# Two attention layers behind a non-local block, split fp32 on one core: shared SBUF regions padded so that large matmul operands begin at 128 modulo 256 bytes

## The chip, the cores and the metric

The kernel runs on one core of a Trainium2 chip. The metric is the device time of one execution in microseconds (us). On-chip memory (SBUF) has 128 partitions; an "address" below is the byte offset of a tensor within a partition, the same in all 128. In the names of this text PE is TensorE, DVE VectorE, ACT ScalarE, POOL GpSimd, and SP the engine that issues the DMAs.

## What is computed

The input is x of 8 batches with 256 tokens of 512 numbers, and a context of the same shape. Cut to what matters:

```python
# first: linear attention over the channels, batch norm folded, residual
W  = einsum('bnc,bcm->bnm', theta_x, phi_x) / 512
x0 = bn(conv(w_w, einsum('bnm,bmc->bnc', W, g_x))) + x
# then (x0 and ctx read as 4 chunks of 512 tokens x 512): two cross-attentions, H=16 heads, K=128
h  = layer_norm(x) * scale + offset
q  = h @ wq + bq ; k, v = ctx @ wk + bk, ctx @ wv + bv    # and one more key and value, bias_k, bias_v
x  = x + softmax(q @ k.T / sqrt(128)) @ v @ wo + bo
# last: an MLP, F=2048
x  = x + gelu(layer_norm(x) @ w_fc1 + b_fc1) @ w_fc2 + b_fc2
```

## The kernel before

Every large product is made of three fp32r matmuls. An operand A is kept as a high part and a low part, A = hi + lo, and `product` (lines 581 to 584) adds lhs.hi x rhs.hi (L582), lhs.hi x rhs.lo (L583) and lhs.lo x rhs.hi (L584) into one PSUM bank. `lhs` is the stationary operand (128 columns, loaded into the array by a weight load of its own, 512 bytes per partition), `rhs` the moving one (512, 258 or 256 columns of 4 bytes). A row of the profile names them as out<-in, both inputs after the arrow; the weight load of the next matmul runs while the present one streams.

The work runs in three stages, in an order that Python writes out by hand (`FRONT`, `SLOTS`, `last_order`), the same for all engines:

- **Front** (K and V of all heads of both layers, into DRAM): `keys` multiplies `wks` (stationary) by `cT` (moving, the transposed context), `values` multiplies `cT` (stationary) by `wvs` (moving). ACT and DVE write the split result into `stage`, four slots in turn, and SP stores each slot to `kd` or `vd`. The non-local block is woven in between.
- **Attention** (64 steps of 4 items each, an item being one head of one 256-token half): `projected` makes q of the next step (stationary `wqs` for even groups of heads, `wqs_b` for odd, moving `hT`), `logits` multiplies `qT` (stationary) by a key block `kb` (moving, 258 columns), `turn` transposes the probabilities, `weighted` multiplies a value block `vb` (stationary) by `PT` (moving, 256 columns), and `output` multiplies `oT` (stationary) by `wos` (moving, 512). Key and value blocks come back from DRAM into two buffers each, `kb0`/`kb1` and `vb0`/`vb1`.
- **Tail** (MLP, 32 steps): `projected` again (`wqs` or `wqs_c` by turns, four steps each) and `output` with `gT0` or `gT1` by turns of one step (stationary) and `wos` or `wos_c` by turns of four steps (moving).

Six stretches of SBUF are shared by tensors that live at different times. `region(name, size)` (line 200) allocates one, and `at(first, size, ...)` (line 204) lays tensors out in it one behind the other. Each tensor or region starts where the one before it ends, so that a region's size decides the addresses of all that come after. `x` starts at byte 16512, which is 128 modulo 256; `turned_rows`, `raw0`, `raw1` and `weights_a` have sizes that are multiples of 256, and so start at 128 as well. `weights_b`, `staged` and `block_0` have 16512 bytes, 128 over a multiple of 256, and halves of 8256 bytes, 64 over one.

Of the kernel before, what the change touches and what calls it, by code (L numbers as in the profile page):

```python
# [28 lines left out]
F32 = mybir.dt.float32  # L29
F32R = mybir.dt.float32r  # L30
# [4 lines left out]
B, TOK, D = 8, 256, 512  # L35
# [5 lines left out]
CH = D // P  # L41
# [144 lines left out]
def bass_xattn(nc, x_in, ctx_in, thw, thb, pgw, pgb, www, bncol, wa, wk, wv, wb, hcol, vrow,  # L186
               lncol, f1col, orow, out):
    ctx = ExitStack()
    with ctx:
        def sb(name, shape, dt=F32):  # L190
            return ctx.enter_context(nc.sbuf_tensor(name, [P, *shape], dt))

        def sem(name):
            return ctx.enter_context(nc.semaphore(name))
# [4 lines left out]

        def region(name, size):  # L200

            return sb(name, [size // 4]), nc.sbuf_base - size

        def at(first, size, *tensors):

            made, where = [], first
            for name, shape, dt in tensors:
                made.append(nc.alloc_sbuf_tensor_at(name, [P, *shape], dt, offset=where))
                where += 4 * int(np.prod(shape))
            assert where <= first + size  # L210
            return made


        x = sb("x", [TILES, D])
        assert (nc.sbuf_base - 4 * TILES * D) % 64 == 0
        _, r = region("turned_rows", 65536)
        cT, hT = at(r, 65536, ("cT", [2, CH, 2048], F32R)) + at(r, 65536, ("hT", [2, CH, 2048], F32R))
        raw = [sb(f"raw{i}", [CH, 256]) for i in range(2)]
        _, r = region("weights_a", 16384)
        (wks,) = at(r, 16384, ("wks", [2, CH, 512], F32R))  # L220
        wqs, wos = at(r, 16384, ("wqs", [2, CH, 256], F32R), ("wos", [2, 2, D], F32R))
        _, r = region("weights_b", 16512)
        (wvs,) = at(r, 16512, ("wvs", [2, CH, 512], F32R))
        kb1, vb1 = at(r, 8256, ("kb1", [2, 2, 516], F32R)) + at(r + 8256, 8256, ("vb1", [2, 4, 256], F32R))
        wqs_c, wos_c = at(r, 8256, ("wqs_c", [2, CH, 256], F32R)) + at(r + 8256, 8256, ("wos_c", [2, 2, D], F32R))
        _, r = region("staged", 16512)
        (stage,) = at(r, 16512, ("stage", [4, 2, 516], F32R))
        (PT,) = at(r, 8256, ("PT", [2, 2, 512], F32R))
        (oT,) = at(r + 8256, 8256, ("oT", [2, 2, 512], F32R))
        _, r = region("block_0", 16512)  # L230
        kb0, vb0 = at(r, 8256, ("kb0", [2, 2, 516], F32R)) + at(r + 8256, 8256, ("vb0", [2, 4, 256], F32R))
        xb, pg, th, wm, msb = at(r, 16512, ("xb", [2, D], F32), ("pg", [4, 256], F32), ("th", [D], F32),
                                 ("wm", [TOK], F32), ("msb", [P], F32))
        gT = at(r, 8256, ("gT0", [2, 2, 512], F32R)) + at(r + 8256, 8256, ("gT1", [2, 2, 512], F32R))
        _, r = region("queries", 8192)
        (qT,) = at(r, 8192, ("qT", [2, 2, 512], F32R))
        wth, wpg, www_s, pgb_s = at(r, 8192, ("wth", [2, CI], F32), ("wpg", [2, 2 * CI], F32), ("www_s", [TOK], F32),
# [3 lines left out]
        _, r = region("spare", 10240)  # L241
# [42 lines left out]
        unit, free, hi, staged = sem("unit"), sem("free"), sem("hi"), sem("staged")  # L284
# [896 lines left out]
```

## Time and profile before

| | |
|---|---|
| median of 3 runs | 2394.86 us (2382.49 to 2408.23) |
| the profiled execution | 2395.99 us, span of its instructions 2394.1 us |
| PE busy | 2351.6 us, 98% |
| PE weight loads | 1997.9 us, 83% |
| DVE busy | 1339.3 us, 56% |
| ACT busy | 1143.8 us, 48% |
| POOL busy | 462.4 us, 19% |
| granted clock of PE | 0.996 of full speed |

Each matmul of `product` has three lines, L582 to L584, by which the profile groups them. The end of a matmul is modelled by the profiler, so durations of neighbours overlap: a matmul of 512 columns shows about 0.39 us and its successor starts 0.23 us after it. The distance from start to start is what counts for time.

### The profile page before, as it was taken

How to read it: one execution, taken by the hardware profiler on the slowest of the kernel's cores; microseconds unless marked ns; L12 is line 12 of the kernel's file. 1: busy time of each engine (PE TensorE's matmuls, PEld its weight loads, DVE VectorE, ACT ScalarE, POOL GpSimd, SP SyncE). 2: the span in 40 equal slices, each digit the busy share in tenths (PEclk: the TensorE clock that was granted, in tenths of full speed). 3: DMA queues.
4: the chain of work that ended last, by engine and by line, in shares of the span. 5: the costliest groups of instructions: out<-in, count | busy, mean ns of one | idle time of the engine just before them, and what ended most of it. 6: DMA issues, size and time to landing. Idle time of an engine off the chain costs nothing.

```text
span 2394.1 us, 32423 instructions
## 1 busy us (share of the span) xinstructions
PE 2351.6 (98%) x12304; PEld 1997.9 (83%) x12304; DVE 1339.3 (56%) x2328; ACT 1143.8 (48%) x2717; POOL 462.4 (19%) x280
## 2 busy tenths in 40 slices
PE   8999999999999899999999989999999999999999
PEld 7888888888888788888888878888888887788887
DVE  4544445445445666666666676666666666644433
ACT  3222222222223566666666677666666667422222
POOL 2121112112123501111001244111001115611110
PEclk9999999999999999999999999999999999999999
DMA  7555656566556424333333333333333331100001
GB/s 272 197 196 203 230 195 215 202 217 227 191 203 212 168 98 143 127 115 136 125 137 124 124 107 119 133 116 134 126 139 124 123 134 45 44 18 27 27 1 70
DMA packets 142168, 331.83 MB, mean 139 GB/s; under 512 B 8896, under 2 KB 74944, under 8 KB 125632
## 3 DMA queue, kind: packets, MB, share of 16 engines
q1 hardware_dynamic: 141296, 329.68, 39.3%
q8 instruction: 99, 1.62, 0.3%
q14 instruction: 53, 0.43, 0.1%
q10 hardware_dynamic: 720, 0.10, 0.0%
HBM read 190.81 MB, written 138.94 MB: 138 GB/s over the span
## 4 chain that ended last, share of the span: by engine, by line
PE 90%; DVE 4%; ACT 4%; DMA 1%; issue 1%; POOL 1%; ACTq 0%; SPq 0%; DVEq 0%; POOLq 0%
PE U L582 23%; PE U L584 23%; PE U L583 23%; PE T L676 4%; PE O L582 2%; PE O L584 2%; PE O L583 2%; PE S L584 2%; PE S L583 2%; PE S L582 2%; DVE hT L1005 1%; ACT aff L815 1%; DVE gT L1015 1%; ACT probs L856 1%; ACT hT L818 1%
## 5 line engine op out<-in xcount | busy, mean ns | idle before, releaser
L1024 DVE TENSOR_TENSOR x<-x,U 128x512 f32<-128x512 f32 x384 | 260.9, 683 | 79.9 <-PE U L584 77.5
L848 ACT ACTIVATE probs<-S,nm 128x257 f32<-128x257 f32 x512 | 237.7, 476 | 37.4 <-DVE nm L1032 37.4
L1032 DVE TENSOR_REDUCE nm<-S 128x2 f32<-128x514 f32 x256 | 177.3, 692 | 123.6 <-PE S L584 119.8
L866 ACT ACTIVATE PT<-T 128x512 fp32r<-128x512 f32 x256 | 152.5, 596 | 173.9 <-PE T L676 173.4
L856 ACT ACTIVATE probs<-probs,rs 128x256 f32<-128x256 f32 x512 | 230.1, 500 | 1.4 <-DVE rs L1036 1.1
L797 ACT ACTIVATE stage<-U,hc 128x512 fp32r<-128x512 f32 x128 | 88.1, 689 | 286.9 <-PE U L584 286.9
L989 DVE SCALAR_TENSOR_TENSOR stage<-U,hc,stage 128x512 fp32r<-128x512 f32 x128 | 96.2, 751 | 223.4 <-ACT stage L797 223.4
L582 PE MATMUL U<-cT,wks 128*128 128x512 f32 x512 | 214.0, 418 | 2.0 <-DVE cT L967 2.0
L582 PE MATMUL U<-wos,oT 128*128 128x512 f32 x512 | 214.2, 418 | 0.4 <-DVE oT L1047 0.4
L804 ACT ACTIVATE stage<-tmp 128x512 fp32r<-128x512 f32 x128 | 81.0, 633 | 271.1 <-DVE tmp L997 271.1
L1047 DVE SCALAR_TENSOR_TENSOR oT<-O,hc,oT 128x256 fp32r<-128x256 f32 x256 | 123.8, 484 | 147.5 <-ACT oT L875 147.3
L464 POOL CAST wos<-raw 128x1024 fp32r<-128x1024 f32 x20 | 20.8, 1039 | 954.1 <-PE U L584 954.1
L584 PE MATMUL U<-wos,oT 128*128 128x512 f32 x512 | 203.0, 397 | 0.0
L583 PE MATMUL U<-wos,oT 128*128 128x512 f32 x512 | 202.1, 395 | 0.0
L582 PE MATMUL U<-wvs,cT 128*128 128x512 f32 x512 | 201.7, 394 | 0.0
L584 PE MATMUL U<-cT,wks 128*128 128x512 f32 x512 | 200.4, 391 | 0.0
L583 PE MATMUL U<-cT,wks 128*128 128x512 f32 x512 | 200.2, 391 | 0.0
L584 PE MATMUL U<-wvs,cT 128*128 128x512 f32 x512 | 199.4, 390 | 0.0
L583 PE MATMUL U<-wvs,cT 128*128 128x512 f32 x512 | 199.4, 389 | 0.0
L1040 DVE TENSOR_TENSOR PT<-T,PT 128x512 fp32r<-128x512 f32 x256 | 175.5, 685 | 42.3 <-ACT PT L866 42.3
L875 ACT ACTIVATE oT<-O,hc 128x256 fp32r<-128x256 f32 x256 | 121.2, 473 | 130.8 <-PE O L584 130.6
L676 PE MATMUL T<-ident,probs 128*128 128x128 f32 x1024 | 155.3, 274 | 13.5 <-ACT probs L856 13.4
(166 smaller groups left out, 5827.1 us busy)
## 6 DMA issues: line engine op xcount, KB each, us to landing
kd<-stage SPq DMA_DIRECT2D x128, 516.0 KB, 3.1
kb<-kd SPq DMA_DIRECT2D x64, 1032.0 KB, 4.8
vd<-stage SPq DMA_DIRECT2D x128, 512.0 KB, 3.2
vb<-vd SPq DMA_DIRECT2D x64, 1024.0 KB, 5.0
raw<-wa SPq DMA_DIRECT2D x24, 512.0 KB, 5.9
raw<-wb SPq DMA_DIRECT2D x24, 512.0 KB, 5.9
raw<-wk SPq DMA_DIRECT2D x16, 512.0 KB, 5.9
raw<-wv SPq DMA_DIRECT2D x16, 512.0 KB, 5.7
```

The costliest lines, as they stand in the source:

```text
L582: pe.matmul(o, lhs[0], rhs[0], start=start, stop=False)
L583: pe.matmul(o, lhs[0], rhs[1], start=False, stop=False)
L584: return pe.matmul(o, lhs[1], rhs[0], start=False, stop=stop)
L676: mm = pe.transpose(T[:, at_:at_ + P], probs[:, J % 2, qt, tt * P:tt * P + P], ident[:])
L848: ins = act.activation(probs[:, r, qt, 0:257], S[:, qt, 0:257], ACT.Exp, bias=nm[:, r, qt:qt + 1], scale=-1.0, accum_out=sums[:, r, qt:qt ...
L856: ins = act.activation(probs[:, r, qt, 0:256], probs[:, r, qt, 0:256], ACT.Copy, scale=rs[:, r, qt:qt + 1])
L866: act.activation(PT[:, J % 2, 0, :], T[:], ACT.Copy).then_inc(pt_hi, 1)
L875: act.activation(oT[:, 0, h, b * 256:b * 256 + 256], O[:, 0:256], ACT.Identity, bias=hc[:, 3, at_:at_ + 1]).then_inc(o_hi, 1)
L1024: dve.tensor_tensor(x[:, tile, :], x[:, tile, :], bank(what, s, t), ALU.add).then_inc(free, 1)
L1032: dve.tensor_reduce(nm[:, J % 2, :], S[:, :, 0:257], AX.X, ALU.min).then_inc(least, 1)
L1040: dve.tensor_tensor(PT[:, J % 2, 1, :], T[:], f(PT[:, J % 2, 0, :]), ALU.subtract).then_inc(pt, 1)
L1047: dve.scalar_tensor_tensor(out=oT[:, 1, h, to], in0=O[:, 0:256], scalar=hc[:, 3, at_:at_ + 1], in1=f(oT[:, 0, h, to]), op0=ALU.add, op1=AL ...
```

## The change

Three regions grow from 16512 to 16640 bytes, which is a multiple of 256, and the tensors in them change places so that a tensor of 8192 bytes comes first and one of 8256 or 8192 second, with nothing between. `region` now asserts that what it made starts at 128 modulo 256. No instruction is added, removed or moved: every engine issues the same operations on the same shapes in the same order with the same waits. Only addresses differ. They come out as follows, in bytes modulo 256:

| tensor | used as | before | after |
|---|---|---|---|
| cT, hT, wks, wvs, wqs, wqs_c, wos, x, raw | both kinds | 128 | 128 |
| kb0, kb1 (moving; their rows have 2064 bytes) | first row | 128 | 128 |
| vb0, vb1 | stationary | 192 | 128 |
| wos_c | moving | 192 | 128 |
| PT | moving | 0 | 128 |
| oT | stationary | 64 | 128 |
| gT0 / gT1 | stationary | 128 / 192 | 128 / 128 |
| qT | stationary | 0 | 128 |
| wqs_b | stationary | 0 | 128 |
| stage, z, aff, tmp, probs | not of `product` | 0 | 128 |
| ident (moving of the transposes) | | 32 | 160 |

A slice of a tensor other than `kb` begins a multiple of 256 bytes behind the tensor's start, so the table holds for each matmul. A row of `kb` is 516 numbers, 2064 bytes or 16 over a multiple of 256, and the second batch half starts 1032 bytes (8 over) further: the eight slices that `logits` reads from it start at 128, 136, 144, 152, 160, 168, 176 and 184, before and after.

```diff
         def region(name, size):
 
-            return sb(name, [size // 4]), nc.sbuf_base - size
+            made = sb(name, [size // 4])
+            assert (nc.sbuf_base - size) % 256 == 128
+            return made, nc.sbuf_base - size
...
-        _, r = region("weights_b", 16512)
-        (wvs,) = at(r, 16512, ("wvs", [2, CH, 512], F32R))
-        kb1, vb1 = at(r, 8256, ("kb1", [2, 2, 516], F32R)) + at(r + 8256, 8256, ("vb1", [2, 4, 256], F32R))
-        wqs_c, wos_c = at(r, 8256, ("wqs_c", [2, CH, 256], F32R)) + at(r + 8256, 8256, ("wos_c", [2, 2, D], F32R))
-        _, r = region("staged", 16512)
-        (stage,) = at(r, 16512, ("stage", [4, 2, 516], F32R))
-        (PT,) = at(r, 8256, ("PT", [2, 2, 512], F32R))
-        (oT,) = at(r + 8256, 8256, ("oT", [2, 2, 512], F32R))
-        _, r = region("block_0", 16512)
-        kb0, vb0 = at(r, 8256, ("kb0", [2, 2, 516], F32R)) + at(r + 8256, 8256, ("vb0", [2, 4, 256], F32R))
-        xb, pg, th, wm, msb = at(r, 16512, ("xb", [2, D], F32), ("pg", [4, 256], F32), ("th", [D], F32),
+        _, r = region("weights_b", 16640)
+        (wvs,) = at(r, 16640, ("wvs", [2, CH, 512], F32R))
+        vb1, kb1 = at(r, 16640, ("vb1", [2, 4, 256], F32R), ("kb1", [2, 2, 516], F32R))
+        wos_c, wqs_c = at(r, 16640, ("wos_c", [2, 2, D], F32R), ("wqs_c", [2, CH, 256], F32R))
+        _, r = region("staged", 16640)
+        (stage,) = at(r, 16640, ("stage", [4, 2, 516], F32R))
+        PT, oT = at(r, 16640, ("PT", [2, 2, 512], F32R), ("oT", [2, 2, 512], F32R))
+        _, r = region("block_0", 16640)
+        vb0, kb0 = at(r, 16640, ("vb0", [2, 4, 256], F32R), ("kb0", [2, 2, 516], F32R))
+        xb, pg, th, wm, msb = at(r, 16640, ("xb", [2, D], F32), ("pg", [4, 256], F32), ("th", [D], F32),
                                  ("wm", [TOK], F32), ("msb", [P], F32))
-        gT = at(r, 8256, ("gT0", [2, 2, 512], F32R)) + at(r + 8256, 8256, ("gT1", [2, 2, 512], F32R))
+        gT = at(r, 16640, ("gT1", [2, 2, 512], F32R), ("gT0", [2, 2, 512], F32R))[::-1]
```

## Rows read from the trace of the kernel before

**Rows 1.** The page: the chain that ended last, by engine, as shares of the span.
```profile
PE 90%; DVE 4%; ACT 4%; DMA 1%; issue 1%; POOL 1%; ACTq 0%; SPq 0%; DVEq 0%; POOLq 0%
```
**Rows 2.** Busy time of PE by stretch: instructions, granted clock, DMA share, GB/s.
```profile
0.00:50.00 50.00, 41.12 (x198) 1.00 0.79 283
50.00:800.00 750.00, 748.68 (x3304) 1.00 0.58 206
800.00:850.00 50.00, 38.03 (x206) 0.86 0.34 127
850.00:2050.00 1200.00, 1186.10 (x7128) 1.00 0.35 122
2050.00:2394.00 344.00, 337.71 (x1473) 1.00 0.09 31
```
**Rows 3.** Waits of PE, longest first: us in total, times, longest.
```profile
PE T L676 <- ACT probs L856: 13.4, 16, 2.9
PE S L716 <- DMA x<-ctx_in: 6.8, 1, 6.8
PE U L619 <- DVE hT L1005: 6.0, 1, 6.0
```
**Rows 4.** Line L583 on PE: duration in ns, minimum/median/maximum, first and last start.
```profile
L583 PE MATMUL U<-cT,wks x512: 387/389/628, 13.1 to 739.3; 128*128 128x512 f32 x171
L583 PE MATMUL U<-wvs,cT x512: 387/389/397, 63.4 to 792.9; 128*128 128x512 f32 x171
L583 PE MATMUL S<-kb,qT x512: 278/282/420, 784.0 to 2017.2; 128*128 128x258 f32 x171
L583 PE MATMUL O<-PT,vb x512: 276/279/416, 800.7 to 2031.7; 128*128 128x256 f32 x171
L583 PE MATMUL U<-wos,oT x512: 387/392/632, 810.0 to 2037.0; 128*128 128x512 f32 x171
L583 PE MATMUL U<-hT,wqs x384: 387/389/398, 766.4 to 2335.5; 128*128 128x512 f32 x192
L583 PE MATMUL U<-hT,wqs_b x256: 387/393/404, 870.9 to 1997.5; 128*128 128x512 f32 x128
```
**Rows 5.** Lines L584 and L582 on PE, same columns.
```profile
L584 PE MATMUL U<-wos,oT x512: 387/394/632, 810.2 to 2037.2; 128*128 128x512 f32 x171
L582 PE MATMUL U<-wos,oT x512: 388/397/776, 809.7 to 2036.7; 128*128 128x512 f32 x171
```
**Rows 6.** Timeline of PE in the tail: start us, duration us, instruction.
```profile
2313.98 0.39 PE L582 MATMUL U<-wos,gT 128*128 128x512 f32 x1
...
2319.42 0.39 PE L582 MATMUL U<-hT,wqs 128*128 128x512 f32 x1
...
2324.86 0.40 PE L582 MATMUL U<-wos,gT 128*128 128x512 f32 x1
...
2330.46 0.39 PE L582 MATMUL U<-hT,wqs 128*128 128x512 f32 x1
```
**Rows 7.** Timeline of PE later in the tail, `wos_c` moving.
```profile
2357.87 0.40 PE L582 MATMUL U<-wos_c,gT 128*128 128x512 f32 x1
...
2363.38 0.40 PE L582 MATMUL U<-hT,wqs_c 128*128 128x512 f32 x1
...
2368.87 0.39 PE L582 MATMUL U<-wos_c,gT 128*128 128x512 f32 x1
...
2374.35 0.39 PE L582 MATMUL U<-hT,wqs_c 128*128 128x512 f32 x1
```
**Rows 8.** The page: DMA issues from SP, KB each, median us to landing.
```profile
vd<-stage SPq DMA_DIRECT2D x128, 512.0 KB, 3.2
```
**Rows 9.** Waits of the SP queue: us in total, times, longest.
```profile
SPq L409 <- DVE stage L1000: 290.9, 127, 7.9
```

## The prediction

> **What bounds the kernel now.** I read first the chain that ended last: PE holds 90% of it [rows 1]. The table by stretch says where PE is not busy: 8.9 us in the first 50 us, 1.3 us in the rest of the front, 12.0 us at the change of stage near 800 us, 13.9 us in the attention and 6.3 us in the tail [rows 2]. The list of PE's waits puts names to them: in total 13.4 us for the probabilities, 6.8 us for the first input, 6.0 us for `hT` [rows 3]. None of these is a steady wait: 16 waits for the probabilities among 256 items are an exception, not the rule. So the kernel's time is the number of matmuls times the distance at which PE starts them, plus about 42 us of gaps. A change that leaves all instructions where they are can act only on that distance (or on the gaps).
>
> **What the distance depends on.** The three lines of a product do the same work on different operands, so their durations can be compared across operands. A duration is the distance to the next start plus a constant: in the tail 24 matmuls `hT,wqs` take 2324.86 - 2319.42 = 5.44 us, 226.7 ns each, and show 389 ns, so the constant is 162 ns [rows 4, 6]. With it, the medians of line L583 (the middle one of a product, whose successor never waits for another engine) sort by address. Where both operands begin at 128 modulo 256 (`cT,wks`, `wvs,cT`, `hT,wqs`), the median is 389 ns, in the front and in the attention alike. `hT,wqs_b` differs from `hT,wqs` only in its stationary tensor, at 0 instead of 128, and takes turns with it in the same loop: 393. `wos,oT`, stationary at 64: 392, and 394 on L584 [rows 4, 5].
>
> The tail has the cleanest comparison, since the same code runs with four pairs of addresses. A step of 24 matmuls from `gT0` (128) with `wos` (128) takes 2319.42 - 2313.98 = 5.44 us; from `gT1` (192) with `wos` (128) 5.60 us [rows 6]. With `wos_c` (192) it takes 5.51 us from `gT0` (128) and 5.48 us from `gT1` (192) [rows 7]. So 128 with 128 is the fastest pair, 192 with 192 nearly so, and unequal residues cost 3 to 7 ns per matmul. This is a real property of where operands lie, of 1 to 3%, and not noise of a wait: none of these steps waits.
>
> The Trainium skill (SBUF — State Buffer, section "SBUF: two separate sides") says that PE never waits on anyone for SBUF, and lists a second, independent read port for weight loads. Taken literally, a matmul's rate could not depend on addresses, and the sum would be 0. The rows on `wqs` and `wqs_b` speak against that reading, and I go by the rows; the rule stays as the second rival below.
>
> **The change part by part.** Against the profiled execution's own 2395.99 us, 1.1 us above the median of the runs:
>
> 1. `cT,wks`, `wvs,cT`, `hT,wqs`, `hT,wqs_c`: same addresses, nothing. That is the whole front (800 us).
> 2. `hT,wqs_b`: 256 x 3 = 768 matmuls, 393 to 389 ns: 768 x 4 = **3.1 us**.
> 3. `wos,oT`: 512 x 3 = 1536 matmuls. L583 gives 3 ns, L584 5 ns; L582's median of 397 mixes in first matmuls of a group, which are late for other reasons. I take 4 ns: **6.1 us**; bounds 3 ns (4.6) and the mean of all three, (8 + 3 + 5) / 3 = 5.3 ns (8.2) [rows 4, 5].
> 4. `gT` in the tail: 32 steps, eight of each pair. Against 5.44 us: 8 x 0.16 + 8 x 0.07 + 8 x 0.04 = **2.2 us** [rows 6, 7].
> 5. `PT,vb`: 1536 matmuls of 256 columns, now 0 with 192, then 128 with 128. No row shows 256 columns with both at 128. Half of 227 ns plus the constant gives 275.5 ns, and the minimum of the row is 276. From 279: 3.5 x 1536 = **5.4 us**. Lower bound: none. I take the full value, as 276 does occur in this row [rows 4].
> 6. `kb,qT`: 1536 matmuls of 258 columns. The same scaling gives 276.4 ns against 282, or 5.6 x 1536 = 8.6 us at most. But only `qT` moves, from 0 to 128; of the eight slices of `kb` seven still start 8 to 56 bytes past 128, so equal residues come about in one of eight. Between 0 and 8.6 I take a quarter, **2.2 us**, since a difference of 8 to 56 bytes is smaller than the 64 that cost `oT` its 3 ns [rows 4].
> 7. Transposes: operands keep their distance (both move by 128). Nothing.
> 8. DMA: `stage` slots start at 0, 32, 64, 96 before and 128, 160, 192, 224 after, and `vb` moves from 192 to 128. What covers a slower store is the ring of four slots: a unit of V is 12 matmuls or 2.7 us, so a slot is needed again after 10.9 us, and the store lands 3.2 us after issue [rows 8]. The queue itself waits for its data, 290.9 us in all [rows 9]. A store would have to take twice as long before PE noticed. Nothing. (The Trainium skill, DMA: Bandwidth & Descriptors, "How a descriptor splits into AXI transactions", says that a descriptor not at a 256-byte boundary costs an extra transaction; by it one slot in four would get 17 for 16 of them. No row here shows that, and the cover above is wide enough for it.)
> 9. ACT, DVE and POOL: the same operations; they are busy for half of the time and PE waits for them rarely [rows 3]. If PE's slot shrinks by 19 us in 1200 us, by 1.6%, their slack does not end.
>
> Sum: 3.1 + 6.1 + 2.2 + 5.4 + 2.2 = 19.0 us. The profiled execution would come to 2377.0, the median of the runs to 2375.9; I say **2376 us**, 0.8% less. The lower end of the sum without the two terms of the short matmuls is 3.1 + 4.6 + 2.2 = 9.9 us (2385); the upper end with all ceilings is 3.1 + 8.2 + 2.2 + 5.4 + 8.6 = 27.5 us (2367).
>
> **Rivals.** (a) The full effect: what counts is that both operands lie within the same stretch, not that they begin at the same byte, so that `kb,qT` reaches 276 ns too. For it: the spread of 278 to 282 to more in its row looks like that of `PT,vb`. Against: seven of eight slices stay unequal. Gain 27.5 us, 2367 us. (b) Nothing: the differences between rows are those of tensors or of places in the code, not of residues, as a rule that PE never waits for SBUF would have it. For it: address pairs are few, and no row has 256 columns at 128 with 128. Against: `gT0` and `gT1` run the same code. 2395 us. (c) Slower: ACT and DVE now write `PT`, `oT`, `qT`, `tmp`, `probs` and `z` all at the residue at which PE reads, where before they were spread over 0, 64 and 192, and each write near PE's read costs it some ns. Its place is the attention stage, with 6,144 matmuls there besides the transposes; it needs 19.0 / 6144 = 3 ns each to undo the gain and 43 / 6144 = 7 ns to make the kernel 1% slower (2419 us). Against it: `hT,wqs` in the attention, amid the same writers, has the same median of 389 as `wvs,cT` in the front [rows 4].
>
> **How the numbers follow.** The likeliest case, a gain of 10 to 24 us, has 0.58; (a) 0.22; (b) 0.15; (c) 0.05. A measurement of this kernel can tell about 1% from no change, which is 24 us, and its three runs lie up to 13 us off their median; this noise is the larger part of my range. Faster by over 1% (below 2371 us) is (a) and the upper edge of the likeliest case: 0.27. Slower by over 1%: 0.04. The rest, 0.69, is within 1%. The range runs from 2361 us, the full effect with some noise, to 2394 us, where the likeliest case's lower end with noise and half of (b) lie.
>
> **What would show it.** In the changed kernel's trace the medians of `hT,wqs_b`, `wos,oT` and all `wos,gT` and `wos_c,gT` on L583 and L584 should be 389 to 390 ns, and tail steps 5.44 us each whatever the buffer. `PT,vb` should fall from 279 to 276; `kb,qT` from 282 to about 281, to 276 under (a). The front's rows must not move. Under (b) `wqs_b` stays at 393; under (c) `hT,wqs` rises above 389 in the attention. If the rows fall as said and the time does not, PE's waits for the probabilities will have grown instead, and I have misjudged the slack.

## The result, and the profile after

The changed kernel takes 2405.5 us (median of 22 runs, 2394.5 to 2408.4), the kernel before 2396.2 us (22 runs beside them, 2382.5 to 2408.2). The ratio is 1.0035, with a 95% interval from 1.0023 to 1.0047: slower by 9.3 us in the medians and by 8.4 us (0.35%) in the ratio, where 2376 us was forecast, and above the upper end of the range (2394 us). The profiled execution takes 2407.6 us, 11.6 us more than that of before.

The times of both kernels come in three groups about 10.5 us apart, near 2386, 2396 and 2407 us, and the result can't be understood without them. Before has 5, 16 and 1 of its 22 runs in them; after has none in the first, 10 in the second (2394.5 to 2400 us) and 12 in the third.

The page of after: busy time, then the chain that ended last.
```profile
PE 2354.0 (98%) x12304; PEld 2003.0 (83%) x12304; DVE 1349.6 (56%) x2328; ACT 1145.0 (48%) x2717; POOL 462.6 (19%) x280
...
PE 89%; DVE 4%; ACT 4%; issue 1%; DMA 1%; POOL 1%; ACTq 0%; SPq 0%; DVEq 0%; POOLq 0%
```
The chain looks like [rows 1]. DVE is busy 10.3 us longer with the same instructions (1339.3 before), and that is the first hint. Busy time of PE by stretch after (columns as in [rows 2]), and then two narrower windows:
```profile
0.00:50.00 50.00, 41.02 (x197) 1.00 0.78 282
50.00:800.00 750.00, 748.60 (x3303) 1.00 0.60 206
800.00:850.00 50.00, 38.04 (x207) 0.86 0.34 128
850.00:2050.00 1200.00, 1177.67 (x7072) 0.99 0.35 121
...
1450.00:1470.00 20.00, 10.39 (x59) 0.75 0.23 80
1470.00:1490.00 20.00, 19.41 (x108) 0.91 0.34 113
```
The front and the change of stage near 800 us are as in [rows 2]. In the attention PE is idle for 22.3 us where it was 13.9 us. One place holds nearly all of the difference: between 1450 and 1470 us PE works 10.4 us of 20. The same two windows of before:
```profile
1450.00:1470.00 20.00, 18.22 (x106) 0.91 0.22 70
1470.00:1490.00 20.00, 20.00 (x121) 1.00 0.44 159
```
The waits of PE after, longest first, name what it waited for there. They stand against [rows 3]: the wait of 6.0 us for `hT` has become two, 14.1 us together, and the wait for the probabilities is as it was.
```profile
PE U L620 <- DVE hT L1006: 14.1, 2, 8.1
PE T L677 <- ACT probs L857: 12.7, 15, 2.8
PE S L717 <- DMA x<-ctx_in: 6.9, 1, 6.9
```
The lines are one higher than before (the `assert`): the middle matmul of a product is L584 now. Its durations after (minimum/median/maximum), to be read against [rows 4] and [rows 5]:
```profile
L584 PE MATMUL U<-cT,wks x512: 387/389/632, 13.2 to 739.9; 128*128 128x512 f32 x171
...
L584 PE MATMUL S<-kb,qT x512: 277/282/420, 784.6 to 2030.0; 128*128 128x258 f32 x171
L584 PE MATMUL O<-PT,vb x512: 277/283/415, 801.3 to 2044.3; 128*128 128x256 f32 x171
L584 PE MATMUL U<-wos,oT x512: 387/393/628, 810.6 to 2049.5; 128*128 128x512 f32 x171
L584 PE MATMUL U<-hT,wqs x384: 387/393/398, 767.0 to 2347.5; 128*128 128x512 f32 x192
L584 PE MATMUL U<-hT,wqs_b x256: 389/393/398, 871.5 to 2010.3; 128*128 128x512 f32 x128
L584 PE MATMUL U<-wos,gT x128: 387/389/628, 2054.1 to 2363.8; 128*128 128x512 f32 x128
```
Four of the five forecast gains are not there: `wqs_b` stays at 393, `oT` goes from 392 to 393, `kb,qT` stays at 282, and `PT,vb` goes the wrong way, 279 to 283. `hT,wqs`, whose addresses did not change, rises from 389 to 393. Only the tail does as forecast. Its timeline after, where each row is the first matmul of a step:
```profile
2326.22 0.39 PE L583 MATMUL U<-wos,gT 128*128 128x512 f32 x1
...
2331.66 0.39 PE L583 MATMUL U<-hT,wqs 128*128 128x512 f32 x1
...
2369.74 0.39 PE L583 MATMUL U<-wos_c,gT 128*128 128x512 f32 x1
...
2375.18 0.39 PE L583 MATMUL U<-hT,wqs_c 128*128 128x512 f32 x1
```
A step takes 5.44 us from either buffer and with either weights, where [rows 6] and [rows 7] have 5.44 to 5.60 us. (Six steps at a change of weights take 5.86 us in after and 5.84 or 5.85 us in before, with a wait of 0.1 us in them.)

### The profile page after: what moved, and what is told of

It is laid out like the page before. It is cut to its first block, busy times and chain, and to the rows that moved or that the text cites. A ratio compares the mean times of both kernels' runs of the same rounds, so it can differ in the third digit from the quotient of the medians.

```text
span 2405.7 us, 32423 instructions
## 1 busy us (share of the span) xinstructions
PE 2354.0 (98%) x12304; PEld 2003.0 (83%) x12304; DVE 1349.6 (56%) x2328; ACT 1145.0 (48%) x2717; POOL 462.6 (19%) x280
## 4 chain that ended last, share of the span: by engine, by line
PE 89%; DVE 4%; ACT 4%; issue 1%; DMA 1%; POOL 1%; ACTq 0%; SPq 0%; DVEq 0%; POOLq 0%
PE U L583 23%; PE U L584 23%; PE U L585 23%; PE T L677 4%; PE O L585 2%; PE O L584 2%; PE O L583 2%; PE S L585 2%; PE S L583 2%; PE S L584 2%; DVE hT L1006 2%; ACT aff L816 1%; ACT probs L857 1%; DVE gT L1016 1%; ACT hT L819 1%
## 5 line engine op out<-in xcount | busy, mean ns | idle before, releaser
L583 PE MATMUL U<-cT,wks 128*128 128x512 f32 x512 | 214.2, 418 | 2.1 <-DVE cT L968 2.1
L583 PE MATMUL U<-wos,oT 128*128 128x512 f32 x512 | 214.7, 419 | 0.2 <-DVE gT L1016 0.2
L584 PE MATMUL U<-wos,oT 128*128 128x512 f32 x512 | 202.6, 396 | 0.0
L583 PE MATMUL U<-wvs,cT 128*128 128x512 f32 x512 | 201.8, 394 | 0.0
L584 PE MATMUL U<-cT,wks 128*128 128x512 f32 x512 | 200.4, 391 | 0.0
L584 PE MATMUL U<-wvs,cT 128*128 128x512 f32 x512 | 199.3, 389 | 0.0
```

What stands on the lines that cost most here:

```text
L583: pe.matmul(o, lhs[0], rhs[0], start=start, stop=False)
L584: pe.matmul(o, lhs[0], rhs[1], start=False, stop=False)
```

## Where the time went: one instruction of DVE that can't get in

Laid over each other, start by start, the two traces are 0.5 us apart at 730 us, 2.0 us at 1426 us and 12.4 us at 1458 us; from there they stay together (12.8 us at 2010 us). The start of the tail adds about 1 us, and its steps give about 2 us back. So 10.4 us of the 11.6 us arise within some 30 us of time. Timeline of after there, first DVE and POOL at the start of the first layer's attention, then at the start of the second layer's, and PE:
```profile
829.61 10.49 DVE L1006 TENSOR_TENSOR hT<-aff,hT 128x512 fp32r<-128x512 f32 x1 [1.64 <-ACT hT L819]
...
824.71 14.84 POOL L537 TENSOR_TENSOR x<-x,brow 128x512 f32<-128x512 f32 x12
...
1453.86 11.84 DVE L1006 TENSOR_TENSOR hT<-aff,hT 128x512 fp32r<-128x512 f32 x1 [1.64 <-ACT hT L819]
...
1449.32 14.85 POOL L537 TENSOR_TENSOR x<-x,brow 128x512 f32<-128x512 f32 x12
1464.13 1.03 POOL L465 CAST wqs_b<-raw 128x1024 fp32r<-128x1024 f32 x1
...
1465.76 1.11 PE L620 MATMUL U<-ident,z 128*128 128x128 f32 x4 [8.12 <-DVE hT L1006]
```
The subtraction that makes the low part of `hT` takes 0.69 us elsewhere, where POOL is idle. Here it takes 10.49 and 11.84 us, and nothing else of DVE runs. POOL meanwhile adds the output bias to `x`, twelve times without a gap. At 829 us DVE ends 0.55 us after POOL's row (824.71 + 14.84 = 839.55, and 829.61 + 10.49 = 840.10). At 1453 us it ends 0.54 us after the cast that follows the row (1465.16 and 1465.70), so it was let in at the first pause that POOL made. PE stands for 8.12 us. Its granted clock is at the lower level of 1.2 GHz (0.50 of full speed) from 1460 us, within this stall, until 1473 us, after it: that is the 0.75 and 0.91 in the windows above.

The same places in the timeline of before:
```profile
829.13 10.46 DVE L1005 TENSOR_TENSOR hT<-aff,hT 128x512 fp32r<-128x512 f32 x1 [1.64 <-ACT hT L818]
...
1451.10 1.50 DVE L1005 TENSOR_TENSOR hT<-aff,hT 128x512 fp32r<-128x512 f32 x1 [1.64 <-ACT hT L818]
...
1456.22 1.79 DVE L1005 TENSOR_TENSOR hT<-aff,hT 128x512 fp32r<-128x512 f32 x1 [1.17 <-ACT hT L818]
...
1445.75 15.86 POOL L536 TENSOR_TENSOR x<-x,brow 128x512 f32<-128x512 f32 x12
```
The first layer had the same lock-out, and it was already the 6.0 us wait of [rows 3]. In the second layer DVE got in twice between two additions, after 1.50 and 1.79 us, and POOL's row became 1.0 us longer (15.86 for 14.84).

The Trainium skill (SBUF — State Buffer, section "Who interferes with whom") says that a DVE instruction with two SBUF inputs contends with a GpSimd instruction that reads SBUF, and that the later one is blocked for the whole instruction. Both traces agree that it is blocked. The second layer of before fits this as it stands, since DVE got in at the end of the addition that it had met. The lock-outs go further: DVE is blocked for a row of up to nine instructions of about 1.25 us, not for one.

One lock-out costs about 10 us, and the groups of times would be executions with none, one and two of them. This is theory A. It says that the addresses decide little by themselves, and that they may act through the moment at which DVE arrives. Theory B is that the new addresses cost time directly: at PE (rival (c) of the prediction, writers near PE's reads), or at DVE, POOL and ACT.

## Experiments

**Are lock-outs the difference?** In both kernels each of POOL's twelve additions in the first two layers waits for an item of the attention, so that they lie apart; `queries` moves behind the first four so that its weights don't come late.

```diff
                 for t in range(4 * c, 4 * c + 4):
+                    if c and n < LAYERS:
+                        pool.wait_ge(logit, n * BODIES * CHUNKS * 4 + t - 3)
                     pool.tensor_tensor(x[:, t, :], x[:, t, :], brow[:], ALU.add).then_inc(ln_bias, 1)
...
-                if E:
+                if E and E != BODIES:
                     queries(E + 1)
...
                         add_bias(n, c)
+                        if c == 1 and n < LAYERS:
+                            queries(E + 2)
```

With the addresses of before:

> The addresses of before, but GpSimd's twelve bias additions at the start of a layer no longer run back to back: each waits for the logits of one item, and the query weights that stood behind them are split earlier. Theory 1 (the loss of the changed kernel is a second DVE instruction that is locked out for 10 us behind GpSimd's additions, and not a slower rate of matmuls): no DVE instruction takes over 3 us at the start of a layer, PE's long waits for hT go, the time falls by 10 to 12 us below the median of before, to about 2385 us, with a spread of runs of under 4 us. Theory 2 (the loss comes from the matmul rate): the additions have nothing to do with it; the time stays within 3 us of before.

With the addresses of after:

> The same spaced additions with the addresses of after. Theory 1: about 2386 to 2388 us, 1 to 3 us above the kernel with spaced additions and the addresses of before (the sum of the steady differences between the two traces), and 18 to 20 us below the changed kernel's 2405.5. Theory 2: it stays 8 to 9 us above the other, whatever that one's time is.

Measured: 2392.5 us with the addresses of before (12 runs, ratio to before 0.9983, interval 0.9970 to 0.9995), and 2392.1 us with those of after (0.9983, 0.9973 to 0.9994). The spread shrinks from 26 us to 8 us with the addresses of before, and from 14 us to 4 us with those of after. The 9 us between the kernels are gone, which is what theory A says and theory B excludes. But the level is not what was expected: 2385 us and a spread under 4 us had been forecast for the first, and it fell by 3.8 us alone. Waits of PE for `hT` in the kernel with after's addresses, against 14.1 us above, and its timeline of DVE at the first layer:
```profile
PE U L624 <- DVE hT L1010: 1.1, 1, 1.1
...
828.15 5.35 DVE L1010 TENSOR_TENSOR hT<-aff,hT 128x512 fp32r<-128x512 f32 x1 [1.64 <-ACT hT L823]
```
One shorter lock-out is left in each, 5.35 us here and 5.85 us with the addresses of before, behind the first additions, which still run in a row. It would account for the missing part of the fall, and the last experiment below takes it away. So the 9 us between the kernels hang on the lock-outs and not on what the addresses do elsewhere: theory A.

**Can the lock-out be aimed?** If the moment of arrival decides, shifting POOL's row should turn the cases round. A scratch addition of 320 columns ahead of the second layer's row in before, of 160 columns in after (shown for before; the scratch tensor is also cleared once at the start):

```diff
+        idle = sb("idle", [320])
...
+                    if n == 1:
+                        pool.tensor_tensor(idle[:], idle[:], idle[:], ALU.add)
                     for c in range(1, CHUNKS):
                         add_bias(n, c)
```

> Addresses of before; one more GpSimd instruction, an addition over 320 scratch columns (about 0.8 us), stands ahead of the twelve bias additions at the start of the second layer and shifts them against DVE by 0.8 us. Theory 1 (whether DVE is locked out is decided by where in an addition of GpSimd's it arrives; in the trace of before 0.35 us after one's start, and it got in; in that of after 0.80 us, and it did not): DVE now meets the additions at another point, 0.8 us earlier in their row, that is near the end of one, and is locked out in most runs; the median goes from 2396 to about 2406 us, as in the changed kernel, with no address changed. Theory 2 (addresses cause the loss): within 2 us of before.

> Addresses of after; the extra GpSimd instruction has 160 columns (about 0.45 us) and moves the additions so that DVE arrives 0.35 us after the start of one, as in the trace of before. Theory 1: mostly the lower of the changed kernel's two groups of times, median about 2397 us. Theory 2: the changed kernel's 2405 us or more.

Measured: 2395.8 us (12 runs, ratio 0.9999, 0.9980 to 1.0019) and 2405.7 us (12 runs, 1.0040, 1.0024 to 1.0055). About 2406 and 2397 us had been expected, and neither came. The delayed before was merely spread over the groups: 4 runs at 2386 to 2387 us, 6 at 2394 to 2398 and 2 at 2408. Its profiled execution happened to be one of the fastest, 2387.0 us, and its timeline of DVE shows no long lock-out in either layer:
```profile
829.52 1.44 DVE L1009 TENSOR_TENSOR hT<-aff,hT 128x512 fp32r<-128x512 f32 x1 [1.64 <-ACT hT L822]
...
1447.40 1.81 DVE L1009 TENSOR_TENSOR hT<-aff,hT 128x512 fp32r<-128x512 f32 x1 [1.17 <-ACT hT L822]
```
The timeline of DVE in the delayed after (profiled at 2404.9 us) has both, the second as:
```profile
1451.04 12.09 DVE L1010 TENSOR_TENSOR hT<-aff,hT 128x512 fp32r<-128x512 f32 x1 [1.64 <-ACT hT L823]
```
So the count of lock-outs accounts for the groups (2387.0 with none, 2396.0 for before with one, 2404.9 and 2407.6 with two), but my model of when one happens was wrong. In the traces of all the kernels here DVE got in whenever it came within 0.04 us of an addition's start. Between 0.35 and 0.41 us it went either way, in the two layers of a single execution even. At about 0.20, at 0.54, at 0.68 and from 0.79 to 1.25 us it was shut out, but at 0.93 us it once got in, amid a row. So the moment of arrival within an addition does not decide it.

**What do the addresses do to PE alone?** 56 phases of 24 matmuls each are appended to before, each matmul complete in itself, on data that is there and with results that nobody uses; the stationary and the moving operand start at 0, 64, 128 or 192. In the last 24 phases ACT and DVE write beside them, at residue 0 or 128.

```diff
+            for p, (n, rw, rm, near) in enumerate(PHASES):
+                pe.wait_ge(act_at, p)
+                pe.wait_ge(dve_at, p)
+                for i in range(24):
+                    mm = pe.matmul(S[:, i % 2, 0:n], hT[:, 0, i % 4, start_of(rw):start_of(rw) + P],
+                                   hT[:, 1, i % 2, start_of(rm):start_of(rm) + n], start=True, stop=True)
```

> The kernel of before, followed by 56 phases of 24 matmuls on hT, each phase with one residue of the stationary and one of the moving operand (0, 64, 128, 192), first with 512 and then with 256 columns and nothing else running, then six pairs of residues with ACT and DVE writing to SBUF at residue 0 or at 128. Theory own operands: at 512 columns equal residues take 227 ns, others 229 to 236; at 256 columns with both at 128 it takes 120 ns even with ACT and DVE idle, unequal ones 113 to 117. Theory neighbours: alone, all 256-column pairs take 113 to 114 ns, and 120 appears only beside ACT and DVE, above all at the same residue.

The kernel took 2642.7 us with its phases. Durations by phase, each row over the window of one phase (up to two matmuls of the phase before it are in). L775 is the line of the phases. The pairs are stationary, moving: (0,0), (0,64), (0,128), (64,0) with 512 columns; then (0,64), (128,64), (128,128) with 256.
```profile
L775 PE MATMUL S<-hT x24: 389/389/472, 2384.4 to 2389.7; 128*128 128x512 f32 x24
L775 PE MATMUL S<-hT x25: 388/392/398, 2389.7 to 2395.2; 128*128 128x512 f32 x25
L775 PE MATMUL S<-hT x26: 390/394/404, 2395.2 to 2401.0; 128*128 128x512 f32 x26
...
L775 PE MATMUL S<-hT x25: 390/394/394, 2406.4 to 2412.0; 128*128 128x512 f32 x25
...
L775 PE MATMUL S<-hT x25: 279/279/283, 2475.8 to 2478.7; 128*128 128x256 f32 x25
...
L775 PE MATMUL S<-hT x26: 276/276/280, 2498.4 to 2501.3; 128*128 128x256 f32 x26
L775 PE MATMUL S<-hT x26: 274/283/283, 2501.2 to 2504.1; 128*128 128x256 f32 x26
```
From start to start, over the last 21 of each phase, 512 columns take 227 ns where both residues are equal (226.7 to 228.5, whichever residue it is), 229 where the moving one is 64 higher, and 232 to 233 in the other two cases. That is the effect that the prediction read from the tail, and it is real. With 256 columns the order turns round. Equal residues are the slowest, 119.6 to 119.8 ns; 128 apart gives 118.4 to 118.7; 64 apart gives either 117.8 or 113.3 to 114.1, and the two are not a matter of the pair: (64,128) takes 117.8 alone and once beside the writers, and 113.3 in its other phase beside them. In the 24 phases with ACT and DVE writing beside PE, at 0 or at 128, no pair is slower than alone by more than 1 ns ((128,128) with 512 columns takes 227.2 and 227.8, against 228.2 alone). So writers that store at the residue at which PE reads cost it nothing here, which is what rival (c) needed.

The phase (128,128) with 512 columns also shows how long that takes. Its distances run 228, 229, 234, 236, 224, 231, 235, 229, 232, 231, and only then 227, 226, 227; (64,64) and (192,192) settle after five. A product in the attention is issued in groups of 6 between shorter matmuls, a step of the tail in groups of 24. In the attention of after, `hT,wqs` and `hT,wqs_b`, all at 128 now, both run through their six matmuls at 234, 233, 231, 230, 230 and 229 ns on average (from each start to the next): the products have equal residues there, and are over before the pace has settled.

**Do the residues of `PT` and `vb` count in the kernel?** Three kernels with the addresses of before except: `vb` at 0 as `PT` is, `vb` alone at 128, and `PT`, `oT` and `vb` all at 128 (this one with one more wait of ACT at the start, since `PT` then overlaps a third slot of `stage`). The lines are shown for `vb0`; `vb1` moves alike.

```diff
-        kb0, vb0 = at(r, 8256, ("kb0", [2, 2, 516], F32R)) + at(r + 8256, 8256, ("vb0", [2, 4, 256], F32R))
+        kb0, vb0 = at(r, 8256, ("kb0", [2, 2, 516], F32R)) + at(r + 8320, 8192, ("vb0", [2, 4, 256], F32R))  # both at 0
+        vb0, kb0 = at(r, 16512, ("vb0", [2, 4, 256], F32R), ("kb0", [2, 2, 516], F32R))  # 0 with 128, both at 128
+        (PT,) = at(r + 128, 8256, ("PT", [2, 2, 512], F32R))  # both at 128
+        (oT,) = at(r + 8320, 8256, ("oT", [2, 2, 512], F32R))
```

> Addresses of before, except vb0 and vb1: at 0 instead of 192, so that PT,vb has 0 with 0. Theory own operands, as in the phases (256 columns with equal residues settle at 120 ns): the mean distance of PT,vb goes from 116.3 to between 118 and 119, near the 118.6 of the changed kernel, its L584 and L583 medians from 279 to 282 or 283. If only 128 with 128 were slow: it stays at 279.

> Addresses of before, except vb0 and vb1 at 128 (PT stays at 0), half way round. The phases have 118.7 ns for this pair when it runs long; so PT,vb should lie between before and the changed kernel, at 117.5 to 118.7 ns.

> Addresses of before, except PT, oT, vb0 and vb1, all at 128; qT, wqs_b, z, aff, probs and the tail as before. Own operands: PT,vb as in the changed kernel (mean distance 118.6 ns, medians 280 to 283); wos,oT about 231.0 as in the changed kernel, and not 227. hT,wqs rises too if what a group of six inherits from the short matmuls before it counts, since neither its own operands nor qT change.

One run each: 2412.1, 2400.4 and 2402.5 us. The kernel with both at 0 has two long lock-outs (11.28 and 11.90 us), the other two kernels one. Line L583 in the kernel with both at 128, and then of `hT,wqs` in the kernel where `vb` alone moved, to 128:
```profile
L583 PE MATMUL O<-PT,vb x512: 274/282/415, 800.8 to 2038.2; 128*128 128x256 f32 x171
L583 PE MATMUL U<-wos,oT x512: 387/393/628, 810.1 to 2043.5; 128*128 128x512 f32 x171
...
L583 PE MATMUL U<-hT,wqs x384: 387/393/398, 765.0 to 2339.9; 128*128 128x512 f32 x192
```
A mean distance below is taken from start to start, without the stretches of low clock; another way of averaging moves it by up to 1 ns. The mean distance of `PT,vb` is 118.4 ns at equal residues (at 0 and at 128 alike), 118.6 with 0 and 128, and 116.3 in before, 64 apart. These 2 ns times 1536 are 3.3 us; with one lock-out each, the two kernels lie 4.4 and 6.5 us above the 2396.0 of before. `wos,oT` with both at 128 stays at 393, so the third term of the prediction fails on its own too. And `hT,wqs` goes from 389 to 393 in all three, though neither its operands nor any tensor that ACT, DVE or POOL write moved in the kernels with `vb` alone. So the rise of `hT,wqs` in after comes from the matmuls of `PT,vb` between its groups, and not from writers beside PE.

**Do the other tensors' addresses matter?** The addresses of after with 128-byte pads that put `z`, `aff` and `probs` back to 0. (`tmp` and `wqs_b` stay at 128, since the region that holds them does.)

```diff
+        pad0 = sb("pad0", [32])
         z = sb("z", [4, D])
         aff = sb("aff", [2, 512])
+        pad1 = sb("pad1", [32])
...
+        pad2 = sb("pad2", [32])
         probs = sb("probs", [2, 2, 258])
```

> The changed kernel with z, aff and probs, which ACT and DVE write and which are no operands of a product, back at residue 0; all products as in the changed kernel. Theory neighbours (rival c of the prediction): hT,wqs in the attention falls back from its mean of 391.7 ns towards the 391.1 of before and its L584-to-be median from 393 to 389, and PT,vb from 281.5 back to 278.5. Theory own operands: both stay as in the changed kernel within 0.3 ns.

One run: 2405.5 us, with two lock-outs of 10.44 and 11.83 us. `PT,vb` stays at 282 to 283 ns on its three lines (279 in before) and `hT,wqs` at 390 to 394 (389 to 392 in before), so neither goes back, as it would under rival (c). The time lies in after's group, so these three tensors need not be at 128 for a second lock-out. One run does not tell how often it comes.

**A version that keeps the good part.** The spaced kernel with the addresses of before, where only the three tensors that end at equal residues with 512 columns move: `gT1` and `wos_c` in the tail, and `wqs_b`.

```diff
-        wqs_c, wos_c = at(r, 8256, ("wqs_c", [2, CH, 256], F32R)) + at(r + 8256, 8256, ("wos_c", [2, 2, D], F32R))
+        wqs_c, wos_c = at(r, 8256, ("wqs_c", [2, CH, 256], F32R)) + at(r + 8192, 8256, ("wos_c", [2, 2, D], F32R))
...
-        gT = at(r, 8256, ("gT0", [2, 2, 512], F32R)) + at(r + 8256, 8256, ("gT1", [2, 2, 512], F32R))
+        gT = at(r, 8256, ("gT0", [2, 2, 512], F32R)) + at(r + 8192, 8256, ("gT1", [2, 2, 512], F32R))
...
-        (wqs_b,) = at(r, 10240, ("wqs_b", [2, CH, 256], F32R))
+        (wqs_b,) = at(r + 128, 10112, ("wqs_b", [2, CH, 256], F32R))
```

> Spaced additions, addresses of before, and only three tensors moved to 128: gT1 and wos_c in the tail, wqs_b in the attention; PT, oT, qT, vb, stage, z, aff, tmp and probs stay. If residues act as the prediction had it for these three: 2.2 us less in the tail and 3 us less for wqs_b, 5 us below the kernel with spaced additions alone. If the rate in the attention depends on what ACT and DVE do beside PE, as the changed kernel's trace suggests: 2 us less from the tail, and between 0 and 2 us from wqs_b.

Measured: 2389.1 us (7 runs, ratio 0.9962, 0.9947 to 0.9977), 3.4 us less than the spaced kernel, within the 2 to 4 us of the second expectation and short of the 5 us of the first. `wqs_b` goes from 233.1 to 229.7 ns here, with `PT,vb` and `wos,oT` around it as before, and the tail's `wos,gT` and `wos_c,gT` are at 227.

**The last lock-out, first try.** All sixteen additions spaced; those of the first chunk go behind the normalisation of all four.

```diff
-                    if c and n < LAYERS:
-                        pool.wait_ge(logit, n * BODIES * CHUNKS * 4 + t - 3)
+                    if t and n < LAYERS:
+                        pool.wait_ge(logit, n * BODIES * CHUNKS * 4 + t)
...
             normalise(0, 1)
-            add_bias(0, 0)
             normalise(0, 2)
             queries(1)
             normalise(0, 3)
-            for c in range(1, CHUNKS):
+            for c in range(CHUNKS):
                 add_bias(0, c)
```

> The kernel with spaced additions and three tensors moved, and now all sixteen additions of a layer's start spaced by one item each and put behind the normalisation. In the kernel with twelve spaced, DVE still took 5.9 us for one hT at 829 us, behind the first four additions. Theory 1: that instruction falls to under 2.5 us, PE loses its low clock around 838 us, and the time falls by a further 4 to 7 us, to about 2383 us. Rival: GpSimd's normalisation of z holds the port as well and hT still waits; the time stays at 2389.

Measured: 2407.4 us (6 runs, ratio 1.0054, 1.0037 to 1.0072). Its waits of PE, and its timeline of DVE:
```profile
PE U L586 <- DVE hT L1009: 27.7, 3, 15.7
...
1453.08 0.69 DVE L1028 TENSOR_TENSOR x<-x,U 128x512 f32<-128x512 f32 x1 [10.96 <-POOL x L538]
1453.68 3.57 DVE L1009 TENSOR_TENSOR hT<-aff,hT 128x512 fp32r<-128x512 f32 x1
```
It had been expected at 2383 us. DVE adds the first outputs to `x` only when the bias of the whole chunk is in, and now waits 10.96 us for that. The two long stalls of PE (15.7 us at the first layer, 11.5 us at the second) are longer than those of a lock-out, and mostly from another cause: the first chunk's semaphore, which I had moved. A short lock-out of 3.57 us follows each of the waits.

**Second try.** Back to the three-tensor kernel, with only the waits of the twelve additions three items later:

```diff
-                        pool.wait_ge(logit, n * BODIES * CHUNKS * 4 + t - 3)
+                        pool.wait_ge(logit, n * BODIES * CHUNKS * 4 + t)
```

> Twelve spaced additions and three tensors moved, as in the kernel that took 2389.1 us, and each addition waits for the logits of three items more, so that the first three of them no longer follow the four additions ahead of them without a gap (in that kernel DVE's hT at 829 us took 6.4 us behind such a row). Theory 1: that hT falls under 2.5 us, no stall of PE for hT at 829 us, time 2384 to 2386 us, the level of the fastest runs of before. Theory 2 (the row has nothing to do with it): 2389 us.

Measured: 2382.8 us (5 runs, 2381.6 to 2385.2; ratio to before 0.9944, 0.9930 to 0.9957). It had been expected at 2384 to 2386 us. It beats both kernels, before by 13.3 us and after by 23 us; about 3.4 us of this are the three tensors, and the rest is the spacing. Timelines of DVE and of POOL, and PE's window around the first layer's start:
```profile
827.89 2.70 DVE L1009 TENSOR_TENSOR hT<-aff,hT 128x512 fp32r<-128x512 f32 x1 [1.65 <-ACT hT L822]
...
823.76 6.28 POOL L538 TENSOR_TENSOR x<-x,brow 128x512 f32<-128x512 f32 x5
834.03 1.27 POOL L538 TENSOR_TENSOR x<-x,brow 128x512 f32<-128x512 f32 x1 [3.99 <-PE S L588]
...
800.00:870.00 70.00, 62.88 (x372) 0.98 0.40 144
```
Five additions in a row instead of twelve: DVE finishes 0.55 us after the fifth ends (830.04 and 830.59 us), and the longest wait of PE for `hT` is 0.4 us. PE is busy for 62.88 us of these 70 where both kernels have 57.9 and 58.0, and the granted clock is 0.98 instead of 0.90.

## Why the prediction was wrong, point by point

- **Front (step 1)**: right. `cT,wks` and `wvs,cT` stay at 389 ns.
- **`wqs_b` (step 2)**: mis-sized. 4 ns were taken; the mean distance fell by 1.1 (232.0 to 230.9 ns), 0.8 us. Two kernels with the same addresses differ by as much: the spaced kernel, with those of before, has 233.1. The step assumed that residues alone made the gap between 393 and 389. But in groups of 6 a product never settles, and its pace depends on what ran before it: unchanged, `hT,wqs` rose by 0.6 ns (228.9 to 229.5). The kernel before had a row that could have warned, since on its last line `hT,wqs`, with both operands at 128, shows 392 and not 389:
```profile
L584 PE MATMUL U<-hT,wqs x384: 388/392/398, 766.6 to 2335.7; 128*128 128x512 f32 x192
```
- **`oT` (step 3)**: mis-sized. 4 ns were taken and 0.4 came (231.4 to 231.0), 0.6 us instead of 6.1. The durations of 392 to 397 in [rows 5] were not a matter of `oT`'s residue.
- **Tail (step 4)**: right. The steps take 5.44 us from every pair of tensors, and they give back about 2.1 us of the forecast 2.2.
- **`PT,vb` (step 5)**: wrong in sign. The step scaled the pace of 512 columns to 256 and got 275.5 ns for equal residues. It is 283 when settled. The mean distance rose from 116.3 to 118.7 ns, 3.7 us lost instead of 5.4 won. The minimum of 276 that I leaned on belongs to operands 64 apart, which is what before had; its row could not show that, as I had said that no row has this case.
- **`kb,qT` (step 6)**: 0.3 ns instead of 1.4 (120.1 to 119.8), 0.5 us. Rival (a) is out.
- **Transposes and DMA (steps 7 and 8)**: nothing came of them; no wait of PE after names a transfer that [rows 3] did not.
- **ACT, DVE, POOL (step 9)**: this step failed too, and it turned a change of nothing into a loss. It counted their busy shares, and passed over one DVE instruction of 10.46 us among hundreds of about 0.69 us, though its trace was there and [rows 3] named its wait. The same instruction stands a second time in the second layer, and there it was locked out for 11.84 us in after. That the new addresses brought this about by shifting DVE's arrival (PE's start is 1.5 us later after 700 us of attention) is not shown.

The sum by measured terms: steps 2, 3, 4 and 6 win 0.8 + 0.6 + 2 + 0.5 us, steps 5 and the rise of `hT,wqs` (0.6 ns x 1152, 0.7 us) lose 4.4 us. That is 0 within an error of two or three microseconds. The two traces laid over each other say the same: without the 10.4 us, the attention loses 1.9 us and the steps of the tail win 2.1. So does the pair of spaced kernels (2392.5 and 2392.1 us). On top come the lock-outs. If a group is one lock-out, before has (16 + 2) / 22 = 0.82 of them per run and after (10 + 24) / 22 = 1.55; the difference of 0.73 times 10.5 us is 7.7 us, of the 0.35% or 8.4 us measured.

So the miss of 29 us between 2376 and 2405.5 has two parts. The larger, some 19 us, is the pace: steps 2, 3, 5 and 6 carried a pace that holds for long runs of equal matmuls with 512 columns over to groups of six and to 256 columns, and of the 16.8 us that they promised, in sum nothing came. Without any change in the lock-outs the kernel would have stayed near 2396 us, outside the range as well. The smaller, 8 to 9 us, is step 9, and it gives the result its sign.

Of the rivals, (b), no effect of addresses on PE, was right in the sum of PE's terms though not in its reason. Rival (c) named the right sign, and its mark, a rise of `hT,wqs` above 389 ns in the attention, is in the rows of after. Its mechanism is not there: the phases show no cost of writers, and moving `vb` alone brings the same rise. The sign was luck. Neither had the lock-out, although the three times of before, 26 us apart, showed that something of this size came and went; I took them for noise and let them widen the range on the wrong side.

What stays open: why after is shut out in the second layer more often than before. In the two traces its DVE arrives 4.54 us into POOL's row instead of 5.35 us, but two attempts to move that moment did not steer the outcome. Open too is by what mechanism residues change PE's pace. And the number of lock-outs is seen only in the one profiled execution of each kernel; for the other runs it is inferred from their times.

## What to carry to other kernels

Look for single instructions that take many times the duration of their group, and not at means and busy shares alone; a long row of GpSimd instructions without a pause beside DVE instructions with two SBUF inputs on the critical path is such a place, and it is cured by spacing the row, with an eye to who waits for its first results. Where runs of the same kernel lie in groups, find what they are made of before costing a change that is smaller than their distance. A pace measured for one shape and a long run of equal matmuls should not be scaled to another shape or to short groups.

## What the runs showed of the hardware that I had not expected

- A DVE `tensor_tensor` with both inputs in SBUF took up to 12.09 us, over eight to nine back-to-back POOL additions of about 1.25 us (and a cast behind them in the second layer), and ended 0.55 us after the first pause. When it gets in behind the addition that it meets it takes 0.9 to 1.8 us, and with POOL idle 0.69 us.
- The pace of fp32r matmuls depends on where the operands start modulo 256 bytes: 227, 229 or 233 ns with 512 columns, with equal residues the fastest; 113 to 120 ns with 256 columns, with equal residues the slowest. Equal residues needed five to ten matmuls to reach 227 ns after a phase with other ones, and short groups of one product changed pace when another product between them did (389 to 393 ns). The Trainium skill (SBUF — State Buffer, section "SBUF: two separate sides") has PE never wait on anyone; these paces differ with no other engine at work, so it need not be waiting on one, and what it is was not found.
- A stall of 8.1 us cost PE more than its length, 10.4 us in all: the granted clock was 0.75 and 0.91 over the two stretches of 20 us from 1450 us, where the kernel before has 0.91 and 1.00.
